# A fused convolution, scan and attention kernel: search one tick late, five shared banks with one burst over the states, and GpSimd's product tied to the next tick's scan

## The reference, cut to what matters

```python
def step(h, inp):                       # 128 inner channels, 16 states each, 4096 steps
    d_t, u_t, b_t, c_t = inp
    h = jnp.exp(d_t[..., None] * A) * h + (d_t * u_t)[..., None] * b_t[:, None, :]
    y = jnp.einsum('bdn,bn->bd', h, c_t)
    return (h, y)
...
y = (jnp.moveaxis(ys, 0, 1) + x * D) * jax.nn.silu(z)
return y @ out_proj_w
...
energy_s = jnp.einsum('bcn,bcm->bnm', q, k)          # 4096 x 4096 for each image
attn_s = jax.nn.softmax(energy_s, axis=-1)
out_s = jnp.einsum('bcm,bnm->bcn', v, attn_s)
```

## Time and profile before

| | us |
|---|---|
| median of 3 runs | 9002.96 (8994.49 to 9007.99) |
| the profiled execution's own time | 9007.69 |
| its span in the profile | 9005.9 |
| convolutions, until the first scan | 639.3 |
| the first 176 scans | 573.4 |
| 116 chunks (scans 176 to 2032) | 7245.8 |
| the rest | 547.4 |

### The profile page before, as it was taken

How to read it: one execution, slowest core, us unless ns; L and a number is a source line. 1 busy time by engine, 2 the same in 40 slices (tenths; PEclk the granted TensorE clock), 3 DMA queues, 4 the chain that set the end, 5 groups by cost and what they waited for, 6 DMA issues and landing times. The chain is left out here.

```text
span 9005.9 us, 135283 instructions
## 1 busy us (share of the span) xinstructions
PE 8085.0 (90%) x38865; PEld 2124.9 (24%) x39494; DVE 7220.5 (80%) x10982; ACT 6245.7 (69%) x12374; POOL 3213.1 (36%) x2343
## 2 busy tenths in 40 slices
PE   8962499999999999989999999989999999999999
PEld 2210122222222222222222222222222222222222
DVE  1238989888898888888888889888888988888721
ACT  1124577777777777777777777777777777777754
POOL 0015444343443434333434434333434434333300
PEclk9986699999999999999999999999999999999999
DMA  8758877767677767767776767767777777677500
GB/s 126 117 107 208 205 186 184 184 176 187 179 185 180 192 175 188 183 171 191 178 190 177 191 180 186 181 172 187 183 185 182 188 178 192 175 180 182 148 27 10
DMA packets 868046, 1530.07 MB, mean 170 GB/s; under 512 B 403336, under 2 KB 436944, under 8 KB 867280
## 3 DMA queue, kind: packets, MB, share of 16 engines
q1 hardware_dynamic: 864208, 1520.77, 68.4%
q10 hardware_dynamic: 3072, 0.40, 0.0%
HBM read 1326.69 MB, written 176.95 MB: 167 GB/s over the span
## 5 line engine op out<-in xcount | busy, mean ns | idle before, releaser
L1251 POOL TENSOR_TENSOR hst<-hst,cbc 128x512 f32<-128x512 f32 x2048 | 2844.7, 1390 | 4630.5 <-ACT carry L1007 4005.7
L996 ACT ACTIVATE pr<-bank 128x512 f32<-128x512 f32 x4096 | 2224.9, 597 | 1051.5 <-PE bank L880 950.2
L1144 DVE TENSOR_TENSOR_SCAN hst<-dA,carry,bank 128x512 f32<-128x512 f32 x1792 | 2294.0, 1280 | 64.4 <-DVE bank L1134 0.3
L889 PE MATMUL bank<-pr,vt 128*64 128x512 f32 x8192 | 2212.4, 618 | 0.0
L1086 DVE CUSTOM_DVE_ANT_0 gains<-bank,gains 128x512 f32<-128x512 f32 x2048 | 1406.2, 687 | 855.1 <-ACT gains L944 829.9
L1134 DVE TENSOR_TENSOR bank<-lanes,bbc 128x512 f32<-128x512 f32 x2048 | 1680.3, 820 | 74.2 <-DMA lanes<-spread_d 31.4
L1002 ACT ACTIVATE dA<-lanes,small 128x512 f32<-128x512 f32 x2048 | 1489.4, 727 | 235.6 <-DMA lanes<-spread_d 146.5
L880 PE MATMUL bank<-t2q,t2k 128*128 128x512 bf16 x4096 | 1554.6, 380 | 108.5 <-issue 66.5
L829 PE MATMUL bank<-s1kx,s1q 128*128 128x512 bf16 x4096 | 1337.5, 389 | 286.1 <-DVE mxp L1086 248.2
L878 PE MATMUL bank<-s1q,s1k 128*128 128x512 bf16 x3467 | 1329.4, 383 | 136.0 <-ACT pr L996 135.5
L944 ACT ACTIVATE gains<-bank 128x512 f32<-128x512 f32 x2048 | 1235.6, 603 | 187.0 <-PE bank L829 183.0
(11 more groups left out here) (116 smaller groups left out, 5804.9 us busy)
## 6 DMA issues: line engine op xcount, KB each, us to landing
lanes<-spread_d SPq DMA_DIRECT2D x2048, 512.0 KB, 5.3
seqt<-seq_d SPq DMA_DIRECT2D x256, 128.0 KB, 4.4
spread_d<-dsp SPq DMA_DIRECT2D x128, 256.0 KB, 2.0
spread_d<-usp SPq DMA_DIRECT2D x128, 256.0 KB, 2.0
bbc<-bc_d SPq DMA_DIRECT2D x128, 256.0 KB, 3.3
cbc<-bc_d SPq DMA_DIRECT2D x128, 256.0 KB, 3.8
xpad<-in_x SPq DMA_DIRECT2D x64, 256.0 KB, 6.7
ypad<-ypad SPq DMA_DIRECT2D x128, 128.0 KB, 4.1
```

The costliest lines, as they stand in the source:

```text
L889: mm = nc.tensor.matmul(ACC[CH * h:CH * (h + 1), :], vt[:, t, :], pr[:, T % PRING, h, :], start=t == 0, stop=t == KT - 1)
L996: nc.scalar.activation(pr[:, T % PRING, h, :], bank_of(("S", T, h))[:], ACT.Exp).then_inc(S["p_full"], 1)
L1144: nc.vector.tensor_tensor_scan(hst[:, T % HRING, :], dA[:, T % 2, :], DBU[:], carry[:, g:g + 1] if sl % CHUNKS else 0.0, ALU.mult, ALU.add ...
L1251: nc.gpsimd.tensor_tensor(h, h, cbc[:, (T - 1) // GROUPS % 2, :], ALU.mult).then_inc(S["hc_in"], 1)
```

## The change

- The search is skewed. The matmul dif of a tick comes first in TensorE's tick, and its ReLU first in ScalarE's. The matmul max, and the fused maximum that needs both, come one tick later. The max matmul stands behind S0 and S1, and the fused maximum directly behind the scan.
- PV, SUM and the small matmuls follow one another with no bfloat16 matmul in between.
- The sum over the states is no longer made four times in a chunk in a bank of its own. It is a ring use "y": all 16 products are summed in one burst of 16 matmuls (32 instructions) in tick 2 of the next chunk. `hst` has 24 slots for this. VectorE reads the bank in tick 3, at the head of its tick.
- The bank that comes free makes the ring five long.
- GpSimd's product of a tick's states waits for the next tick's DBU in addition to the carry copy.
- `bcs` and `rinv` share the memory of `rest` and `dens`; the copy of the sums (L1015) waits for the "res" matmul's reader of the quarter before.

```diff
-SEARCH_LOAD = [SEARCH - KT + 8 * (p + 1) for p in range(QUARTERS - 1)] + [GROUPS]
+SEARCH_LOAD = [SEARCH - KT + 8 * (p + 1) + 1 for p in range(QUARTERS - 1)] + [GROUPS]
 PRING = 4
-HRING = 8
-BATCH = 4
+HALVES = GROUPS // 2
+HRING = GROUPS + HALVES
...
+def slot_of(T):
+
+    k = T % GROUPS
+    return k if k >= HALVES or T // GROUPS % 2 == 0 else k + GROUPS
...
-        found = self.searches(T)
+        found, last = self.searches(T), self.searches(T - 1)
         if found:
-            t = (T - SEARCH) % KT
-            ev += [("dif", found, t), ("max", found, t)]
+            ev.append(("dif", found, (T - SEARCH) % KT))
+        if last:
+            ev.append(("max", last, (T - 1 - SEARCH) % KT))
...
-        name = {7: "out", 12: "xv", 14: "en"}.get(r)
+        name = {2: "y", 7: "out", 12: "xv", 14: "en"}.get(r)
...
-        uses, plan = self.small_uses(T), []
+        uses = self.small_uses(T)
+        plan = [e for e in uses if e[0] == "dif"]
         if self.attends(T):
             plan += [("S", T, 0), ("S", T, 1)]
+        plan += [e for e in uses if e[0] == "max"]
         if self.attends(T - 1):
             plan.append(("PV", T - 1))
-        plan += uses[0:2]
-        b = T // BATCH - 1
         if T % 2 == 0 and self.attends(T - 1):
             plan.append(("SUM", T // 2 - 1))
-        if T % BATCH == BATCH - 1 and self.scans(BATCH * b):
-            plan.append(("Y", b))
-        return plan + uses[2:]
-
-
-SIGNAL_OF = {"PV": "pv", "SUM": "den", "Y": "y_mm"}
-DVE_USES = ("max", "turn", "mix", "res", "en")
-RING = 4
+        return plan + [e for e in uses if e[0] not in ("dif", "max")]
+
+
+SIGNAL_OF = {"PV": "pv", "SUM": "den"}
+DVE_USES = ("max", "turn", "mix", "res", "en", "y")
+RING = 5
...
-    RB, (DBU, ACC, DEN, YPS) = banks[0:RING], banks[RING:]
-    AUX = RB[0]
+    RB, (DBU, ACC, DEN) = banks[0:RING], banks[RING:]
+    AUX, AUX2 = RB[0], RB[1]
...
-        bcs = sb("bcs", [2 * D_STATE, CHUNK])
+        bcs = rest[0:2 * D_STATE, 0:CHUNK]
-        rinv = sb("rinv", [P, CHUNK])
+        rinv = dens
...
+                        elif kind == "y":
+                            wait(pe, "hc_in", GROUPS * (c + 1) - 1)
+                            for gl in range(GPB):
+                                for j in range(BLOCKS):
+                                    mm = nc.tensor.matmul(
+                                        bank[BLOCK * j:BLOCK * (j + 1), :],
+                                        cst[:, C_SUM + BLOCK * gl:C_SUM + BLOCK * (gl + 1)],
+                                        hst[:, slot_of(GROUPS * c + BLOCKS * gl + j), :],
+                                        start=gl == 0, stop=gl == GPB - 1, tile_position=(0, BLOCK * j))
...
-                    def reduce_states(b):
-
-                        gl = b % GPB
-                        if gl == 0:
-                            wait(pe, "y_in", b // GPB - 1)
-                        wait(pe, "hc_in", BLOCKS * b + BLOCKS - 1)
-                        for j in range(BLOCKS):
-                            mm = nc.tensor.matmul(YPS[BLOCK * j:BLOCK * (j + 1), :],
-                                                  cst[:, C_SUM + BLOCK * gl:C_SUM + BLOCK * (gl + 1)],
-                                                  hst[:, (BLOCKS * b + j) % HRING, :],
-                                                  start=gl == 0, stop=gl == GPB - 1, tile_position=(0, BLOCK * j))
-                        mm.then_inc(S["y_mm"], 1)
...
+                        near = [e for e in sched.small_uses(T) if e[0] == "dif"]
+                        for e in near:
+                            small_use(e)
...
-                        for e in sched.small_uses(T):
+                                           hst[:, slot_of(T - 1), CHUNK - 1:CHUNK]).then_inc(S["carried"], 1)
+                        for e in sched.small_uses(T)[len(near):]:
                             small_use(e)
...
                         if done:
                             wait(act, "st_den", sched.before(done), 16)
                             wait(act, "den", ((T - 1) // 2 - 1,))
+                            taken(act, ("res", sched.before(done)))
                             nc.scalar.copy(dens[:], DEN[:]).then_inc(S["den_in"], 1)
...
-                        if sched.chunk(c) and r == 4:
-                            wait(dve, "y_mm", (GPB * (c + 1) - 1,))
+                        if sched.chunk(c) and r == 3:
+                            full_wait(dve, ("y", c))
                             full_wait(dve, ("out", c - 1))
-                            nc.vector.scalar_tensor_tensor(out=ysb[:], in0=u[:, c % 2, :], scalar=dskip, in1=YPS[:],
-                                                           op0=ALU.mult, op1=ALU.add).then_inc(S["y_in"], 1)
+                            nc.vector.scalar_tensor_tensor(out=ysb[:], in0=u[:, c % 2, :], scalar=dskip, in1=bank_of(("y", c))[:],
+                                                           op0=ALU.mult, op1=ALU.add).then_inc(S["dve_took"], 1)
...
                             if due("da_in", T):
                                 dve.wait_ge(S["da_in"], due("da_in", T))
-                            wait(dve, "y_mm", ((T - HRING) // BATCH,))
+                            full_wait(dve, ("y", sl - 1 if T % GROUPS >= HALVES else sl - 2))
                             nc.vector.tensor_tensor_scan(
-                                hst[:, T % HRING, :], dA[:, T % 2, :], DBU[:],
+                                hst[:, slot_of(T), :], dA[:, T % 2, :], DBU[:],
                                 carry[:, g:g + 1] if sl % CHUNKS else 0.0, ALU.mult, ALU.add).then_inc(S["scan"], 1)
+                        for e in ev:
+                            if e[0] == "max":
+                                small_use(e)
...
                         for e in ev:
-                            small_use(e)
+                            if e[0] != "max":
+                                small_use(e)
...
@@ -1247,13 +1254,14 @@
                                 pool.wait_ge(S["scan"], due("scan", T - 1))
                             if due("carried", T - 1):
                                 pool.wait_ge(S["carried"], due("carried", T - 1))
-                            h = hst[:, (T - 1) % HRING, :]
+                            if due("dbu_in", T):
+                                pool.wait_ge(S["dbu_in"], due("dbu_in", T))
+                            h = hst[:, slot_of(T - 1), :]
                             nc.gpsimd.tensor_tensor(h, h, cbc[:, (T - 1) // GROUPS % 2, :],
                                                     ALU.mult).then_inc(S["hc_in"], 1)
...
-                            if due("y_in", c):
-                                pool.wait_ge(S["y_in"], due("y_in", c))
+                            taken(pool, ("y", c))
```

More of the change, by code:

```diff
@@ L532, in _ @@
                 nc.tensor.matmul(AUX[:, 0:P], wdtt, wdt4, start=True, stop=True).then_inc(wps, 1)
-                nc.tensor.matmul(YPS[0:CH, 0:CH], wvt, wbn2, start=True, stop=True).then_inc(wps, 1)
+                nc.tensor.matmul(AUX2[0:CH, 0:CH], wvt, wbn2, start=True, stop=True).then_inc(wps, 1)
                 nc.tensor.matmul(ACC[:, 0:CH], woutt, wqk, start=True, stop=True).then_inc(wps, 1)
@@ L546, in _ @@
                 nc.scalar.copy(wout[:, CH:P], ACC[:, 0:CH])
-                nc.scalar.copy(wxv[0:CH, CH:2 * CH], YPS[0:CH, 0:CH])
+                nc.scalar.copy(wxv[0:CH, CH:2 * CH], AUX2[0:CH, 0:CH])
         clear(nc, [zeroed, got, capped, made, wps, wdone])
@@ L551, in pipeline @@
                    seq0 seq1 lanes0 lanes1 lanes2 lanes3 da_in
-                   dbu_in scan carried hc_in y_mm y_in y2_in st_x1 kd_in head_in rest_in
+                   dbu_in scan carried hc_in y2_in st_x1 kd_in head_in rest_in
                    mid_in low_in st_bc ld_b ld_c abs_in st_split st_vt ring_full act_took dve_took p_full
@@ L623, in span @@
                 if sched.chunk(c):
-                    for at, n in ((4, "y_in"), (4, "y2_in"), (8, "st_x1"), (8, "kd_in"), (9, "head_in"),
+                    for at, n in ((4, "y2_in"), (8, "st_x1"), (8, "kd_in"), (9, "head_in"),
                                   (10, "rest_in"), (11, "mid_in"), (12, "low_in"), (14, "st_split"), (13, "st_vt")):
@@ L627, in span @@
                             sched.note(n, c)
-                for n, offset in (("max_in", TURN - 2), ("nm3_in", TURN), ("nm_row", TURN + 1), ("acc_in", MAIN + KT),
+                for n, offset in (("max_in", TURN - 1), ("nm3_in", TURN), ("nm_row", TURN + 1), ("acc_in", MAIN + KT),
                                   ("den_in", MAIN + KT + 1),
@@ L696, in _ @@
                             wait(sp, "ld_c", c - 2, 16)
-                            issued(sp.dma_start(bc_d[c % 2], bcs[:]), "st_bc")
+                            issued(sp.dma_start(bc_d[c % 2], bcs), "st_bc")
                         if sched.chunk(c) and r == 12:
@@ L927, in _ @@
                                 sums(e[1])
-                            elif e[0] == "Y":
```

(11 more changed lines are left out.)

## The result

The changed kernel takes 8868.33 us (median of 4 runs, 8863.89 to 8872.16) against 9004.57 for the kernel before: a ratio of 0.985, with a 95% interval of 0.9833 to 0.9867. The gain is 136 us. The direction and the range held, but the size didn't: 284 us were predicted, and less than half came.

What follows compares the result with a forecast made beforehand. TensorE was taken to set the pace. A chunk: -1.1 - 3.5 + 1.8 + 0.4 + 0.3 = -2.1 us, times 116 is -244; with -30 and -10 it is -284, giving 8720 us, range 8500 to 8890.

Steps and rivals of the forecast that it cites:

- TensorE's order: With max ahead of PV, 12 float32 matmuls a chunk lose a 0.09 us entry: 1.1 us less, bounds 0 and 1.4.
- The hold around the table loads: Tick 10, TensorE waiting for ScalarE's exponential around the logarithm: grows from 0.87 to 1.8 us a chunk.
- Ticks 0 to 2: ScalarE has three copies in a row and TensorE shorter ticks: 0.4 us a chunk, bounds 0 and 1.0.
- The holds by VectorE: TensorE waiting for banks the fused maximum has not read: falls to 0.3 us a chunk, bounds 0 and 2.6.
- the coupling that it names: ReLU heading ScalarE's tick needs VectorE's previous tick, so VectorE's lateness reaches exponentials, dA and carry; no separate term.
- the direction of the product's shift: GpSimd's product begun with the scan: DBU's mean falls from 777 to about 690 ns; half of 1.4 us counted.
- The third rival: Slower: the product, kept back by DBU and a later carry, overlaps the next DBU more often; 9290 us, chance 0.08.
- The 59.3 us a chunk of VectorE: VectorE's 54.8 us of work plus 4.5 of waiting in a chunk, against the 61.85 us a chunk takes today.
- The burst: Four groups of state sums issued together behind tick 2's SUM: 4.0 us, costing nothing by itself but using VectorE's slack.
- The first stretch: First 176 scans, no scores made: product behind DBU lowers DBU from 925 to 696 ns; 30 us saved, bounds 0 and 80.
- The tail: 80 SUMs lose the entry of 0.09 us and some holds go: 10 us saved.
- The second rival: VectorE's lateness after the burst passes through ScalarE's ReLU into PV, 3.5 us a chunk stay: 8835 us, chance 0.13.

Runs made afterwards that it cites:

- a_carry1: Changed kernel with ScalarE's carry copy moved from fifth to first instruction of its tick: 8570.65 us.
- a_nolog: Changed kernel with a ReLU in place of the logarithm, so ScalarE loads no table (computation differs): 8805.52 us.
- a_tiny: Changed kernel with GpSimd's product cut to 8 of its 512 columns, waits and signals kept (computation incomplete): 8563.18 us.
- a_both: Changed kernel with ScalarE's carry copy first in its tick and VectorE's read of the burst's bank behind tick 3's scan: 8573.27 us.
- a_ylate: Changed kernel with VectorE's read of the burst's bank in tick 3 behind the scan instead of ahead of DBU: 8745.46 us.

## Why the prediction was right in direction and wrong in size

The quarters of before and after are compared here by start times: every start of a matmul less the start of the one before it, less the unheld step of such a pair, which is 0.22 us between two bfloat16 matmuls. What is left is a hold. Where a matmul has no record in the trace, its step is taken as unheld. In a chunk the holds are (us):

| | tick 10 | all others | together |
|---|---|---|---|
| before | 1.1 | 3.0 | 4.1 |
| after | 1.7 | 2.9 | 4.6 |
| a_carry1 | 1.8 | 0.3 | 2.1 |

**TensorE's order: right.** Predicted -1.1 us a chunk. A float32 matmul started 0.31 us behind a bfloat16 one and a bfloat16 one 0.22, throughout both quarters, and such steps fell from 28 to 16 in a chunk: 12 x 0.09 = 1.1. That the busy time fell by nearly the same, 1.04 (120.3 / 116), doesn't prove it, since busy time also holds waiting.

**The hold around the table loads: too dear, and wrong in worth.** The prediction let it grow from 0.87 to 1.8, by the idle time in brackets; by the same reading it is 1.30. By start times it grew from 1.1 to 1.7. So the growth was 0.4 to 0.6 us, where I had 0.9; that the 1.7 lies beside the 1.8 is a coincidence of two ways to measure. And it isn't 1.7 us of the chunk that could be had: in a_nolog only 0.5 come back, and VectorE's lateness fills 1.2.

**Ticks 0 to 2: too dear.** I had 0.4 us; in the quarter nothing was held there.

**The holds by VectorE: the step that failed.** The prediction says "I let these holds fall to 0.3 us in a chunk", and of the late product "I count half of it, 0.7 us, and on VectorE alone: it is in the 0.3 above". They did not fall: outside tick 10 the holds are 2.9 us a chunk, where they had been 3.0, and all of them but 0.3 end with VectorE's fused maximum. The longest of the quarter:

```profile
7269.56 0.39 PE L834 MATMUL bank<-s1kx,s1q 128*128 128x512 bf16 x1 [1.00 <-DVE mxp L1089]
```

The view of the fused maximum's line says the same of all of the kernel. The weight loads of dif and max waited for it like this before (the changed kernel has 586.5 us in 648 places, shown above):

```profile
  PEld bank L829: 570.0, 670
```

Nor had the prediction a price for the coupling that it names. In the kernel before no wait of a ReLU for the maximum stands in the view; now 833 ReLUs wait, for 698.2 us. That 0.3 us of such holds can be reached is shown by a_carry1, but only with the carry copy moved. Two things were read wrongly.

First, the direction of the product's shift. From the earlier trace rows I saw that product and scan leave each other alone, and concluded that DBU would fall to some 690 to 730 ns. I also noted from the earlier trace rows that the product waits for the carry in 30 of 32 ticks, but took "DBU is long done" from the one tick of the earlier trace rows. Over the 116 chunks the product already lay over the DBU of its tick in 576 of 1856 ticks (counted in the trace). VectorE was often held up by ScalarE's ReLU, at the end of its tick, and so came late against the carry copy. The skew takes exactly that wait away, and puts a ReLU ahead of the carry as well: the carry comes 0.67 us later behind its scan and the next DBU 0.30 earlier, in the median, so that the product often lies over the DBU after that. DBU rose to 914. The third rival names this mechanism and its price, but I gave it 0.08 because "a late VectorE has its DBU later, and then the carry is there first". It did not go slower, because the order, the shorter burst and the freed ReLU wait pay for more than the product costs. Against a_carry1 and a_tiny the overlap costs the changed kernel 298 to 305 us. Part of this was paid before the change too (353 long DBUs then, 458 now); how much the change added isn't known, as no run took the product out of the kernel before.

Second, slack. The 59.3 us a chunk of VectorE came out nearly as said, but from other terms: 56.7 of work and 2.65 of waiting before the burst (5.3 / 2), where I had 54.8 and 4.5. To set VectorE 0.45 us under the pace and price its holds at 0.3 was too bold: work comes in single ticks, and four in a chunk have a DBU of over 1 us, whatever the mean says. With VectorE at 52.8 of work in a chunk of 58.1 (a_carry1), the idle time falls to 1.9 in its quarter, and the chunk of 59.0 us is under the 59.75 of the forecast.

**The burst.** Predicted 4.0 us and no cost of its own. It takes 3.62, and 3.55 to the next start:

```profile
7170.31 1.06 PE L917 MATMUL bank<-pr,ones 128*32 128x512 f32 x8
7171.19 3.62 PE L866 MATMUL bank<-hst,cst 128*32 128x512 f32 x32
7174.74 0.39 PE L834 MATMUL bank<-s1kx,s1q 128*128 128x512 bf16 x1
```

"This lies beside TensorE's work and costs nothing by itself. It uses up slack" is right where slack is (a_both). Where none is, VectorE's standing before it is worth up to 123 us (a_ylate). The four groups took 1.00 us each to the next start when they stood apart, so the burst itself is 0.45 us shorter, which the prediction didn't have. With it the quarter's account closes: -1.1 by the order, -0.45 by the burst and +0.5 by the holds are the -1.05 by which a chunk became shorter (61.85 to 60.80).

**The first stretch.** Predicted -30, measured -0.1. DBU's mean there fell from 925 to 868 ns, not to 696:

```profile
L1137 DVE TENSOR_TENSOR bank<-lanes,bbc 128x512 f32<-128x512 f32 x175 | 151.9, 868 | 31.6 <-DMA lanes<-spread_d 26.0 <-DVE cacc L1166 0.3
L1004 ACT ACTIVATE dA<-lanes,small 128x512 f32<-128x512 f32 x176 | 126.9, 721 | 189.6 <-DMA lanes<-spread_d 132.3 <-DVE hst L1147 56.8
```

175 times 0.057 us is 10 us, and they don't reach the length. The wait alone on the kernel before brings this stretch to 564.9 us, and the carry first on the changed one to 552.1: the gain was there, and it too needs the carry early.

**The tail: right in its number,** -10.0 for -10; what it is made of was not looked at.

The second rival, "3.5 us a chunk stay", was the nearest in its number (8835). Its path is there too: the ReLU's waits for the maximum are the 12.4 us above. Its root was the burst and the late product together: with the skew alone DBU is already at 898 ns, yet taking away either the product's overlap (298 us) or VectorE's wait before the burst (123 us) mends much of it.

**What stays open.** Why the late read (a_ylate) gains 123 us although DBU's mean rises to 983 was only argued. The table shows how long TensorE was held, and not how much of VectorE's lateness came round over ScalarE's ReLU; that was not separated. In the best version the holds of tick 10 remain (1.8 us a chunk); no run has tried to move the logarithm in it.

## What to carry to other kernels

Before pricing a wait that keeps two engines apart, ask which of its inputs comes last today, and whether the rest of the change turns this order round: here an edit that freed VectorE brought it into GpSimd's way, and one copy moved to the head of ScalarE's tick was worth twice the whole change. Two edits can need each other: on the changed kernel less its gate, the wait for DBU (8964), the early carry alone cost 398 us, the gate alone gave 96, and both together gave 394. And where an engine's mean load is within 1% of the pace, as VectorE's was here, look at its long ticks before pricing its holds near nothing.

## What the runs showed of the hardware that was not expected

The price of sharing between VectorE and GpSimd depends on which instructions meet. A product that begins with the scan leaves it at 1.28 us; one that is under way when DBU begins stretches DBU. Over the changed kernel DBU takes between 672 and 1830 ns:

```profile
L1137 DVE TENSOR_TENSOR bank<-lanes,bbc x2048: 672/699/1830, 634.4 to 8383.6; 128x512 f32<-128x512 f32 x187
```

Most of this is the product's: with it cut to 8 columns the mean is 726, and over the 116 chunks 102 DBUs take over 1 us instead of 458. (GpSimd's other instructions stay.) The Trainium skill, page "SBUF — State Buffer", section "SBUF: two separate sides", calls this an exclusive lock that the first to start holds to its end. The trace agrees nearly in the tick of 7222.40: DBU ends 0.56 us behind the product, somewhat less than its own 0.70.

It was new to me how much the same 1.27 us product can cost or not: 8570.65 us for the kernel with every product let in behind the DBU of its tick, and 9362.05 with the same instructions and one wait less.
